# Two cross-attention layers on one core: query parts stored in 8 DMAs and loaded in 3, a row tile's products in parts, row turns one slot on, a last row tile in two column halves

## The chip, the cores and the metric

The kernel runs on 1 core of a Trainium2 chip. The metric is the device time of one launch in microseconds (us). The kernel before takes 1469.72 us, the median of 3 runs (1467.17 to 1472.53). Below, PE is TensorE (matmuls), DVE is VectorE, ACT is ScalarE, POOL is GpSimd, and SP is SyncE, which here only issues DMAs.

## The reference, cut to what matters

```python
def layer0(x, ctx):                        # x (8,100,512), ctx (8,722,512), H = 16 heads of 32
    qn, kn = layer_norm(x) * g1 + b1, layer_norm(ctx) * g1 + b1
    Q, K, V = qn @ wq + bq, kn @ wk + bk, kn @ wv + bv
    out = softmax(Q @ K.T / sqrt(32)) @ V
    x = x + out @ wo + bo
    y = layer_norm(x) * g2 + b2
    return x + gelu(y @ w1 + b1_) @ w2 + b2_
def layer1(q, ctx):                        # H = 16 heads of 64, no biases
    qh, kh, vh = q @ Wq, ctx @ Wk, ctx @ Wv
    out = softmax(qh @ kh.T / 8 - 2) @ vh @ Wfc + q
    return layer_norm(out) * gamma + beta
return layer1(layer0(x, ctx), ctx)
```

## The kernel before

Every fp32 operand of a matmul is split into two fp16 parts (high and low), and a product is three fp16 matmuls: high by high, high by low, low by high.

**Stages.** Attention 0 (0 to 537 us), the two MLP products (537 to 693), attention 1 (693 to 1468). Both attentions are `attention(nc, layer, ...)`. In layer 0 a unit is one of the 8 batches with its 16 heads in 4 groups of 4; in layer 1 there are 16 units (batch, half of the heads) with 2 groups. The work runs in steps: step s projects keys and values of unit s, computes scores and softmax of unit s - 1, and ends what is left of unit s - 2. A step has 24 slots in layer 0 (4 groups times 6 key tiles) and 12 in layer 1, and `Slots` is the table that says in which slot each piece stands. Every engine has its own loop over the same slots, in the same order (`step`), and the engines meet only in semaphores, so an engine that waits in a slot holds everything behind it.

**Scores.** `max_scores` makes a head's scores for the row maximum, `take_max` (DVE) reduces them, `max_transposes` and `place_max` bring the maximum into the query stack; `scores` makes the scores again, turned; `exp` and `prob_hi` (ACT) and `prob_lo` (POOL, in the last groups of layer 0 and in half of layer 1's tiles DVE) make the probabilities' parts; `times_v` multiplies by V. The first `max_scores` of unit u stands in slot 18 of step u. It waits for the unit's queries (`q_loaded`) and for the stacked keys of the first 8 heads (`stacked[0]`).

**The SP queue.** SP issues its DMAs in one written order. Before the steps of layer 0: `store_queries(m)` for four tiles (8 DMAs each: for each of 4 heads the high part, written twice, and the low part), the last two context tiles of batch 2, `queries_stored` (waits until the stores have landed), `place_onehot([1])`, `store_ctxT(1)` (the turned context of batch 1 to DRAM, 1444 KB, for layer 1). Then for unit 1: `load_q` (1 DMA over 96 partitions), `stack_k(.., 0)` and `stack_k(.., 1)` (12 DMAs each), more context tiles, `store_rstd`, `load_rrow`, and so on. Context tile (2, 5) waits until DVE has taken the statistics of tile (2, 1).

**Rows of layer 0.** The output projection, residual and second norm of row tiles 0 to 4 (128 rows each) are done inside the last steps: `row_products` (12 matmuls), `row_sum` with statistics, `row_power_of` (POOL), `row_centre`, `row_final`, `row_hi`, `row_lo`, `row_turn` (8 transposes), `row_copy`. `row_base` gives each tile's first slot, counted from the start of step 7, and `row_acc` to `row_turn` the offsets from it. Tile 4 has base 45, slot 21 of step 8; its bias is added by DVE at the head of its `row_sum`. Step 8 computes no projections any more, step 9 is the last group's `times_v` and the last output turn, and then comes a barrier and the MLP.

**Rows of layer 1.** `close_rows(T, half)` multiplies a row tile by half of Wfc (12 matmuls). In the last step (17) tiles 5 and 6 are left: both halves of tile 5 and the first of tile 6 stand in slot 5, behind the last `times_v`, and the second half of tile 6 in slot 9, behind the last output turn. `sum_rows` and `finish_rows` (DVE) end a tile, and SP stores it.

Of the kernel before, what the change touches and what calls it, by code (L numbers as in the profile page):

```python
# [25 lines left out]
P = 128  # L26
B, SQ, SK, E = 8, 100, 722, 512
ROWS = B * SQ
# [452 lines left out]
class Slots:  # L481
# [4 lines left out]
    def __init__(self, layer):  # L486
# [28 lines left out]
        self.row_base = [3, 9, 15, 21, 45]  # L515
        self.row_place = [4, 9, 13, 17, 18]
        self.row_acc, self.row_sum, self.row_pow, self.row_centre, self.row_final, self.row_hi, self.row_lo, self.row_turn = 0, 2, 3, 3, 4, 5, 7, 8
# [41 lines left out]
def attention(nc, layer, ctx_d, ctxT_d, q_d, w_k, w_v, kb_col, vb_row, ident, ident16, eps, score_bias, outT,  # L559
# [21 lines left out]
    NQ = 1 if layer == 0 else 3  # L581
    QM = queries[1].shape[3] // P
    QPER = 2 * HPT if layer == 0 else 2
# [3 lines left out]
    with Scope(nc, f"attn{layer}") as sc:  # L587
# [132 lines left out]
        if layer == 1:  # L720
# [4 lines left out]
            row_stats, row_mv = sc.sb("row_stats", [P, RT, 6]), sc.sb("row_mv", [P, RT, 2])  # L725
# [57 lines left out]
        def row_bank(T):  # L783
            return (p_proj, p_max)[T // 2 % 2][:, T % 2, :]
# [24 lines left out]
        def _(sp):  # L809
# [33 lines left out]
            def load_q(u, par, b):  # L843
                if not (isinstance(u, int) and u < 2):
                    sp.wait_ge(sc_ready, NSLOT * (u - 1))
                h0 = 0 if layer == 0 else NH * par
                if layer == 0:
                    sp.dma_start(qstack[0][:96, par], q_d[:, h0:h0 + NH, bass.ds(b * SQ, SQ)]).then_inc(q_loaded[par], 16)
                else:
                    part = lambda a: q_d[a, h0:h0 + NH, :, bass.ds(b * SQ, SQ)].rearrange("h p r -> p h r")  # L850
                    sp.dma_start(qstack[0][:DK, par], part(0)).then_inc(q_loaded[par], 16)
                    sp.dma_start(qstack[0][DK:, par], part(0)).then_inc(q_loaded[par], 16)
                    sp.dma_start(qstack[1][:DK, par], part(1)).then_inc(q_loaded[par], 16)
# [18 lines left out]
            def store_queries(m):  # L872

                if layer == 1:
                    sp.wait_ge(q_lo_made, 2 * m + 2)
                if layer == 0:
                    for j in range(HPT):
                        head, rows = HPT * m + j, slice(DK * j, DK * j + DK)
                        sp.dma_start(q_d[0:2 * DK, head, :].rearrange("(o p) (n r) -> p o n r", o=2, n=2),
                                     q_rows(0, m)[rows].rearrange("p (o n) r -> p o n r", o=1).to_broadcast([DK, 2, 2, QHALF])  # L880
                                     ).then_inc(q_stored[m % RING], 16)
                        sp.dma_start(q_d[2 * DK:, head, :].rearrange("p (n r) -> p n r", n=2), q_rows(1, m)[rows]).then_inc(q_stored[m % RING], 16)
                else:
                    for a in range(2):
                        sp.dma_start(q_d[a, HPT * m:HPT * m + HPT].rearrange("h p (n r) -> (h p) n r", n=2), q_rows(a, m)).then_inc(q_stored[m % RING], 16)
# [37 lines left out]
            if layer == 0:  # L923
                def unit(u, prep):
# [32 lines left out]
                    stack_k(u, u % 2, 1)  # L957
                    if u + 2 < U:
# [66 lines left out]
            if layer == 0:  # L1025
                store_ctxT(1)
# [32 lines left out]
        def _(pe):  # L1059
# [139 lines left out]
            def row_products(T):  # L1199
# [4 lines left out]
                pe.wait_ge(proj_freed, row_use(T) - 1)  # L1204
                if T == EARLY - 1:
                    pe.wait_ge(max_made, U * NG * HG)
                last_batch = (r0 + r - 1) // SQ
                pe.wait_ge(misc_freed, sl.misc_count(last_batch + 2, ("out", 0)))
                for k in range(ET):
# [3 lines left out]
                last.then_inc(proj_ready, 1)  # L1213
# [12 lines left out]
            def close_rows(T, half):  # L1226
# [15 lines left out]
                for k in range(ET):  # L1242
                    for i, (a, b) in enumerate(PARTS):
# [1048 lines left out]
```

## Time and profile before

| | us |
|---|---|
| median of 3 runs | 1469.72 (1467.17 to 1472.53) |
| the profiled execution, its own time | 1469.81 |
| its span | 1468.0 |
| PE busy | 1376.9 (94%) |
| DVE busy | 881.4 (60%) |
| ACT busy | 684.9 (47%) |
| POOL busy | 445.5 (30%) |
| mean granted PE clock | 0.982 |

The profile is one execution; its own time is 1.81 us over its span. A row of the timeline gives start, duration, engine, line of the kernel, operation, the tile written and those read, the count of instructions merged in it, and in brackets the idle time just before with what ended it. Matmuls are pipelined, so the work of PE is read from start to start.

### The profile page before, as it was taken

Reading aid. Unit: us, or ns where it says so; the run is one execution under the profiler, and the core shown is the slowest. Engines: PE = TensorE matmul, PEld = TensorE weight load, DVE = VectorE, ACT = ScalarE, POOL = GpSimd, SP = SyncE. Lnnn points to the kernel's source line nnn. Section 1 sums busy time; section 2 is a strip of 40 time slices with the busy share of each in tenths; the row PEclk is TensorE's granted clock in tenths of the full one; section 3 lists DMA queues with packets and bytes.
Section 4 is the critical chain, followed back from the end, with each engine's and each line's share of the span. In section 5 each row is a group of like instructions: output and inputs, shape, how many; then the busy total and the mean of one; then the engine's idle time right before and its main releaser. Section 6 shows DMA issues by size and latency. Waiting matters only on the chain.

```text
span 1468.0 us, 31527 instructions
## 1 busy us (share of the span) xinstructions
PE 1376.9 (94%) x12841; PEld 877.1 (60%) x12841; DVE 881.4 (60%) x1574; ACT 684.9 (47%) x1322; POOL 445.5 (30%) x493
## 2 busy tenths in 40 slices
PE   6988999999998879999999999999999999999997
PEld 4555666666655545544556666666666666666654
DVE  6777778878878748434435544454544445555564
ACT  3556567666755635221224444444444444444431
POOL 3125566666666731200001111112111111211223
PEclk9999999999999879999999999999999999999999
DMA  8226443343454035132433334123333322333421
GB/s 259 65 65 163 138 134 81 117 127 95 139 140 111 9 97 186 58 108 79 145 81 70 102 70 110 41 54 97 70 102 70 103 48 47 104 71 89 99 69 37
DMA packets 118205, 141.38 MB, mean 96 GB/s; under 512 B 49949, under 2 KB 92461, under 8 KB 116013
## 3 DMA queue, kind: packets, MB, share of 16 engines
q1 hardware_dynamic: 116873, 137.10, 34.4%
q8 instruction: 102, 1.67, 0.5%
q10 hardware_dynamic: 1188, 2.27, 0.5%
q14 instruction: 42, 0.34, 0.1%
HBM read 63.15 MB, written 22.17 MB: 58 GB/s over the span
## 4 chain that ended last, share of the span: by engine, by line
PE 47%; DVE 3%; issue 1%; ACT 1%; POOL 0%; POOLq 0%; ACTq 0%
PE attn_p_proj L1103 17%; PE attn_p_proj L1098 14%; PE attn_p_max L1125 3%; PE attn_p_sc L1314 2%; PE attn_p_sc L1156 2%; PE attn_p_sc L1155 2%; PE attn_p_pv L1184 1%; PE attn_p_proj L1244 1%; PE attn_p_pv L1183 1%; PE attn_p_pv L1185 1%; DVE attn_nmax L1692 1%; PE attn_p_max L1244 1%; ACT attn_probs L1460 1%; DVE attn_knat L1725 1%; ACT attn_knat L1489 0%
## 5 line engine op out<-in xcount | busy, mean ns | idle before, releaser
L1692 DVE TENSOR_REDUCE attn_nmax<-attn_p_max 100x1 f32<-100x722 f32 x250 | 226.3, 905 | 143.5 <-PE attn_p_max L1125 141.2
L799 POOL TENSOR_TENSOR attn_probs<-kernel_w_first,attn_probs 128x400 f16<-128x400 f32 x96 | 90.6, 943 | 673.4 <-ACT attn_probs L1460 673.4
L1103 PE MATMUL attn_p_proj<-kv_w_v,attn_ctxT 128*128 128x512 f16 (+1 forms) x1152 | 264.3, 379 | 0.0
L1450 ACT ACTIVATE kernel_w_first<-attn_p_sc,attn_score_bias 128x400 f32<-128x400 f32 x192 | 113.5, 591 | 307.9 <-PE attn_p_sc L1156 307.9
L1098 PE MATMUL attn_p_proj<-attn_ctxT,kv_w_k 128*128 128x361 f16 x1536 | 249.1, 317 | 4.1 <-DVE attn_knat L1725 3.5
L799 POOL TENSOR_TENSOR attn_probs<-attn_p,attn_probs 128x400 f16<-128x400 f32 x186 | 197.8, 1070 | 167.9 <-ACT attn_probs L1460 167.0
L1098 PEld LDWEIGHTS attn_p_proj<-attn_ctxT,kv_w_k 128*128 128x128 f16 x1536 | 144.6, 97 | 88.6 <-DVE attn_knat L1725 9.7
L1103 PEld LDWEIGHTS attn_p_proj<-kv_w_v,attn_ctxT 128*128 128x128 f16 (+1 forms) x1152 | 110.3, 101 | 111.1
L1450 ACT ACTIVATE attn_p<-attn_p_sc 128x400 f32<-128x400 f32 x192 | 96.4, 502 | 154.3 <-PE attn_p_sc L1152 151.6
L1103 PE MATMUL attn_p_proj<-l_w_v,attn_ctxT 128*128 128x512 f16 (+1 forms) x576 | 133.6, 382 | 1.9 <-DVE attn_vbuf L1731 1.8
L1098 PE MATMUL attn_p_proj<-attn_ctxT,kernel_w_first 128*128 128x361 f16 x768 | 127.9, 317 | 0.0
L1725 DVE SCALAR_TENSOR_TENSOR attn_knat<-attn_p_proj,attn_knat 128x361 f16<-128x361 f32 x128 | 68.3, 533 | 70.1 <-ACT attn_knat L1489 69.6
L1731 DVE SCALAR_TENSOR_TENSOR attn_vbuf<-attn_p_proj,attn_vbuf 128x512 f16<-128x512 f32 x96 | 66.2, 690 | 63.3 <-ACT attn_vbuf L1498 61.6
L1460 ACT CAST attn_probs<-attn_p 128x400 f16<-128x400 f32 x192 | 98.8, 519 | 0.0
L1460 ACT CAST attn_probs<-kernel_w_first 128x400 f16<-128x400 f32 x192 | 98.8, 515 | 0.0
L1098 PEld LDWEIGHTS attn_p_proj<-attn_ctxT,kernel_w_first 128*128 128x128 f16 x768 | 71.7, 97 | 37.8 <-issue 1.1
L1156 PE MATMUL attn_p_sc<-kernel_w_first,attn_kstack_b 72*128 72x100 f16 (+1 forms) x768 | 94.0, 208 | 0.0
L1155 PE MATMUL attn_p_sc<-kv_w 128*128 128x100 f16 (+1 forms) x768 | 93.5, 208 | 0.0
L799 DVE TENSOR_TENSOR attn_probs<-kernel_w_first,attn_probs 128x400 f16<-128x400 f32 (+1 forms) x96 | 55.2, 575 | 62.7 <-ACT attn_probs L1460 62.7
L1103 PEld LDWEIGHTS attn_p_proj<-l_w_v,attn_ctxT 128*128 128x128 f16 (+1 forms) x576 | 56.1, 102 | 59.6 <-DVE attn_vbuf L1731 2.6
L1489 ACT ACTIVATE attn_knat<-attn_p_proj 128x361 f16<-128x361 f32 x128 | 60.6, 473 | 62.5 <-PE attn_p_proj L1098 62.5
L1183 PE MATMUL attn_p_pv<-attn_vbuf,attn_probs 128*128 128x65 f16 (+1 forms) x768 | 84.9, 194 | 2.0 <-DVE attn_probs L799 2.0
(259 smaller groups left out, 2595.9 us busy)
## 6 DMA issues: line engine op xcount, KB each, us to landing
kv_w<-attn_knat SPq DMA_DIRECT2D x128, 180.5 KB, 3.5
attn_kstack<-attn_knat SPq DMA_DIRECT2D x192, 90.2 KB, 2.2
ctx_turned<-attn_ctxT SPq DMA_DIRECT2D x8, 1444.0 KB, 8.1
attn_ctxT<-ctx_turned SPq DMA_DIRECT2D x8, 1444.0 KB, 8.4
attn_kstack_b<-attn_knat SPq DMA_DIRECT2D x64, 180.5 KB, 3.6
attn_c<-in_ctx_dram SPq DMA_DIRECT2D x35, 256.0 KB, 3.2
kv_w_v<-in_L_xattn_w_dram SPq DMA_DIRECT2D x7, 1024.0 KB, 5.4
q_parts<-attn_probs SPq DMA_DIRECT2D x16, 200.0 KB, 2.5
```

The lines of the kernel that those rows point to most:

```text
L799: eng.tensor_tensor(probs[:r, g % 2, 1, t, :HG * SQ], p32[:r, t % 3, :], probs[:r, g % 2, 0, t, :HG * SQ], ALU.subtract).then_inc(p_lo_mad ...
L1098: last = pe.matmul(bank[:, :HALF], w_k[:, wa, k, c0 + m * P:c0 + (m + 1) * P], ctxT[:, cpar, ca, k, n * HALF:(n + 1) * HALF], **flags)
L1103: last = pe.matmul(bank[:r, :], ctxT[:, cpar, ca, k, P * t:P * t + r], w_v[:, wa, k, c0:c0 + E], **flags)
L1155: pe.matmul(out, kstack[0][:, par, h, P * t:P * t + r], qstack[0][:, par, h, :], start=True, stop=False)
L1156: last = pe.matmul(out, kstack[1][:MR + 2 * HG, par, h, P * t:P * t + r], qstack[1][:MR + 2 * HG, par, h, :], start=False, stop=True)
L1183: pe.matmul(p_pv[:, o:o + OC], ph, v[:, :OC], start=first, stop=False)
L1450: act.activation(p32[:r, t % 3, :], p_sc[:r, t % 2, :HG * SQ], ACT.Exp, bias=bias_col[:r, 0:1] if score_bias else 0.0).then_inc(exp_made, 1)
L1460: act.copy(probs[:r, g % 2, 0, t, :HG * SQ], p32[:r, t % 3, :]).then_inc(p_hi_made, 1)
L1489: act.activation(knat[:, m, 0, cols], src, ACT.Identity, scale=1.0 / WS).then_inc(k_hi_made, 1)
L1692: dve.tensor_reduce(nmax[:SQ, hh:hh + 1], max_banks(u, g, hh)[:SQ, :, :HALF], AX.XY, ALU.max, negate=True).then_inc(max_made, 1)
L1725: dve.scalar_tensor_tensor(knat[:, m, 1, cols], p_proj[:, a % 2, :HALF], 1.0 / WS, knat[:, m, 0, cols], ALU.mult, ALU.subtract).then_inc(p ...
L1731: dve.scalar_tensor_tensor(vbuf[:r, par, t, :, DK + 1:], p_proj[:r, use(u, a) % 2, :].rearrange("p (h d) -> p h d", d=DK), rstd[:r, par, t ...
```

## The change

1. **Queries of layer 0.** The DRAM tensor is now two parts by head (`q0_parts`), as in layer 1. `store_queries` issues 2 DMAs a tile, 8 in all, instead of 32. `load_q` issues 3 DMAs of 32 partitions for a unit (the high part twice, the low part once) instead of 1 of 96.
2. **`store_ctxT(1)`** moves from before the units to behind unit 1's second `stack_k`.
3. **Row turns of layer 0** stand one slot on (`row_turn` 8 to 9), and `row_copy` with them.
4. **Row tile 4**: base 45 to 42; its 12 matmuls are done 3 each in slots 16 to 19 of step 8, its bias is added in slot 17, its sum in slot 20, its turn in slot 3 of step 9.
5. **Layer 1**: `close_rows(5, 0)` moves from slot 5 to slot 0 of step 17. Tile 6 is computed in two halves of 256 columns in two banks, and its sum and statistics are taken for each half.

```diff
-        self.row_base = [3, 9, 15, 21, 45]
+        self.row_base = [3, 9, 15, 21, 42]
+        self.last_acc = {16: 0, 17: 1, 18: 2, 19: 3}
+        self.last_bias_t = 17
-        ... self.row_turn = 0, 2, 3, 3, 4, 5, 7, 8
+        ... self.row_turn = 0, 2, 3, 3, 4, 5, 7, 9
@@ load_q
-                if layer == 0:
-                    sp.dma_start(qstack[0][:96, par], q_d[:, h0:h0 + NH, bass.ds(b * SQ, SQ)]).then_inc(q_loaded[par], 16)
+                low = qstack[0][2 * DK:3 * DK, par] if layer == 0 else qstack[1][:DK, par]
+                sp.dma_start(qstack[0][:DK, par], part(0)).then_inc(q_loaded[par], 16)
+                sp.dma_start(qstack[0][DK:2 * DK, par], part(0)).then_inc(q_loaded[par], 16)
+                sp.dma_start(low, part(1)).then_inc(q_loaded[par], 16)
@@ store_queries
-                    for j in range(HPT):
-                        ...
+                for a in range(2):
+                    sp.dma_start(q_d[a, HPT * m:HPT * m + HPT].rearrange("h p (n r) -> (h p) n r", n=2), q_rows(a, m)).then_inc(q_stored[m % RING], 16)
@@ unit (SP, layer 0)
                     stack_k(u, u % 2, 1)
+                    if u == 1:
+                        store_ctxT(1)
@@ step (PE)
-                    if sl.row_tile(s, j, sl.row_acc) is not None:
+                    if layer == 0 and s == U - 1 and sl.row_tile(s, j, sl.row_acc) is not None:
                         row_products(sl.row_tile(s, j, sl.row_acc))
+                    if layer == 0 and s == U and j in sl.last_acc:
+                        row_products(EARLY - 1, range(sl.last_acc[j], sl.last_acc[j] + 1))
+                    if layer == 1 and s == U + 1 and j == 0:
+                        close_rows(RT - 2, 0)
                     if layer == 1 and s == U + 1 and j == PV_T + HG - 1:
-                        close_rows(RT - 2, 0)
                         close_rows(RT - 2, 1)
@@ row_cols
+            if T == RT - 1:
+                return [(slice(E // 2 * i, E // 2 * (i + 1)), p_max[:, i, :E // 2]) for i in range(2)]
@@ sum_rows
+                for i, (cols, bank) in enumerate(row_cols(T)):
+                    dve.wait_ge(rows_ready, T + i + 1)
+                    dve.scalar_tensor_tensor(res[T][:r, cols], bank[:r], 1.0 / WS, res[T][:r, cols], ALU.mult, ALU.add).then_inc(rows_summed, 1)
+                    dve.wait_ge(rows_summed, T + i + 1)
+                    dve.bn_stats(row_stats[:r, T + i, :], res[T][:r, cols]).then_inc(row_stats_made, 1)
@@ step (DVE)
+                    if layer == 0 and s == U and j == sl.last_bias_t:
+                        last_row_bias(EARLY - 1)
```

SP's queue from the end of the query stores to unit 1's keys, before; the first row is the last of 32 stores (`q_stack`), `attn_c` are context tiles, `attn_kstack<-attn_kstack` is `place_onehot`, `ctx_turned` is `store_ctxT(1)`, `attn_qstack<-q_stack` is `load_q(1)`, and the last row the 24 DMAs of `stack_k`.

```order
L882 DMA q_stack<-attn_kstack 32x800
L817 DMA attn_c<-in_ctx_dram 128x512
L817 DMA attn_c<-in_ctx_dram 82x512
L921 DMA attn_kstack<-attn_kstack 8x2888 x4
L836 DMA ctx_turned<-attn_ctxT 128x5776
L848 DMA attn_qstack<-q_stack 96x16x100
L899 DMA attn_kstack<-attn_knat 32x2x722 x24
```

The same stretch after:

```order
L879 DMA q_parts<-attn_kstack 128x800 x8
L821 DMA attn_c<-in_ctx_dram 128x512
L821 DMA attn_c<-in_ctx_dram 82x512
L915 DMA attn_kstack<-attn_kstack 8x2888 x4
L853 DMA attn_qstack<-q_parts 32x16x100
L854 DMA attn_qstack<-q_parts 32x16x100
L855 DMA attn_qstack<-q_parts 32x16x100
L893 DMA attn_kstack<-attn_knat 32x2x722 x24
L840 DMA ctx_turned<-attn_ctxT 128x5776
```

32 stores have become 8, one query load three, and the 1444 KB store stands behind the 24 key DMAs.

DVE at the end of step 8 and in step 9 before: `attn_ctxT<-attn_ctxT,attn_rrow` is the bias of row tile 4, `attn_probs` is `prob_lo`, `attn_ctxT<-attn_p_proj` the head of `row_sum`, `82x400` the last tile of the last group.

```order
L1786 TENSOR_TENSOR attn_ctxT<-attn_ctxT,attn_rrow 128x512
L1789 SCALAR_TENSOR_TENSOR attn_ctxT<-attn_p_proj,attn_ctxT 128x512
L1791 BN_STATS attn_stats<-attn_ctxT 128x6
L1793 BN_AGGR attn_mv<-attn_stats 128x2
L1795 TENSOR_SCALAR attn_mid_rstd<-attn_mv 128x1
L799 TENSOR_TENSOR attn_probs<-attn_p,attn_probs 82x400
```

After, the end of the same stretch:

```order
L1804 SCALAR_TENSOR_TENSOR attn_c<-attn_ctxT,attn_mv 128x512
L803 TENSOR_TENSOR attn_probs<-attn_p,attn_probs 128x400
L1811 SCALAR_TENSOR_TENSOR attn_c<-attn_c,attn_mid_rstd,attn_ctxT 128x512
L1741 COPY attn_pv_sb<-attn_p_pv 100x260
L1743 RECIPROCAL attn_orecip<-attn_pv_sb 100x4
L803 TENSOR_TENSOR attn_probs<-attn_p,attn_probs 82x400
```

The bias and the sum with its statistics stood ahead of the last `prob_lo`; now they are slots earlier, and `row_centre` and `row_final` stand ahead of it instead.

PE at the end of layer 1 before: `60x512` is row tile 5, `100x512` tile 6, `attn_misc` the last output turn.

```order
L1244 MATMUL attn_p_proj<-kernel_w_qo,kernel_x_parts 60x512 x12
L1244 MATMUL attn_p_proj<-kv_w_k,attn_out_o_upper 60x512 x12
L1244 MATMUL attn_p_max<-kernel_w_qo,kernel_x_parts 100x512 x12
L1196 MATMUL attn_misc<-kernel_ident,kv_w 128x100 x8
L1244 MATMUL attn_p_max<-kv_w_k,attn_out_o_upper 100x512 x12
```

After, the same place; tile 5's first half has gone ahead of the 72 matmuls of `times_v` that stand before these rows:

```order
L1241 MATMUL attn_p_proj<-kv_w_k,attn_out_o_upper 60x512 x12
L1241 MATMUL attn_p_max<-kernel_w_qo,kernel_x_parts 100x256 x24
L1190 MATMUL attn_misc<-kernel_ident,kv_w 128x100 x8
L1241 MATMUL attn_p_max<-kv_w_k,attn_out_o_upper 100x256 x24
```

## Rows read from the trace of the kernel before

**Rows 1.** Waits of PE, whole run; engine, tile, line <- releaser: us, times, longest
```profile
PE attn_misc L1133 <- DVE attn_nmax_parts L1701: 9.2, 17, 2.5
...
PE attn_misc L1223 <- DVE attn_cparts L1815: 5.6, 5, 2.0
PE attn_p_max L1125 <- issue: 5.3, 1, 5.3
PE attn_p_pv L1180 <- DVE attn_probs L799: 4.9, 1, 4.9
```

**Rows 2.** Timeline of SP, 104 to 150 us; start, duration, engine, line, transfer
```profile
105.25 0.59 SPq L879 DMA_DIRECT2D q_stack<-attn_kstack  x1
105.88 0.42 SPq L882 DMA_DIRECT2D q_stack<-attn_kstack  x1
...
125.53 2.77 SPq L921 DMA_DIRECT2D attn_kstack<-attn_kstack  x4
...
130.54 18.87 SPq L899 DMA_DIRECT2D attn_kstack<-attn_knat  x24
```

**Rows 3.** Layer 1's query stores and loads; ns min/median/max, first and last start
```profile
L885 SPq DMA_DIRECT2D q_parts<-attn_probs x16: 512/619/1435, 701.1 to 730.0; - x16
...
L853 SPq DMA_DIRECT2D kernel_w_first<-q_parts x16: 634/635/1576, 736.1 to 1361.0; - x16
```

**Rows 4.** Timeline of DVE, 112 to 116 us; start, duration, line, tiles
```profile
113.23 0.68 DVE L1650 BATCH_NORM_STATS2 attn_stats<-attn_c 128x6 f32<-128x512 f32 x1
...
115.56 0.96 DVE L1684 SCALAR_TENSOR_TENSOR attn_knat<-attn_kscaled,l_kb_col,attn_knat 128x722 f16<-128x722 f32 x1
```

**Rows 5.** Timeline of PE, 125 to 150 us, around the wait of step 1
```profile
125.09 0.49 PE L1125 MATMUL attn_p_max<-attn_kstack,attn_qstack 96*100 96x361 f16 x2
...
128.79 0.51 PE L1125 MATMUL attn_p_max<-attn_kstack,attn_qstack 96*100 96x361 f16 x2
...
143.35 0.81 PE L1125 MATMUL attn_p_max<-attn_kstack,attn_qstack 96*100 96x361 f16 x2 [5.33 <-issue]
...
149.29 0.47 PE L1125 MATMUL attn_p_max<-attn_kstack,attn_qstack 96*100 96x361 f16 x2
```

**Rows 6.** DMA issues; count, KB each, median us to landing
```profile
kv_w<-q_parts SPq DMA_DIRECT2D x32, 100.0 KB, 3.0
...
attn_qstack<-q_stack SPq DMA_DIRECT2D x7, 300.0 KB, 8.3
...
ctx_turned<-attn_ctxT SPq DMA_DIRECT2D x8, 1444.0 KB, 8.1
```

**Rows 7.** Timeline of DVE in step 8, behind the row turn
```profile
491.49 0.91 DVE L1692 TENSOR_REDUCE attn_nmax<-attn_p_max 100x1 f32<-100x722 f32 x1
```

**Rows 8.** Timeline of PE in step 8, row tile 4's products
```profile
519.12 3.35 PE L1211 MATMUL attn_p_proj<-kernel_w_qo,kernel_x_parts 128*128 128x512 f16 x12
522.31 0.35 PE L1152 MATMUL attn_p_sc<-attn_qstack,attn_kstack 104*128 104x100 f16 x4
```

**Rows 9.** Windows of step 8; length, busy us by engine, clock, DMA
```profile
506.50:520.00 13.50, 11.25 (x126) 8.88 (x127) 7.27 (x13) 9.85 (x22) 9.73 (x13) 0.51 0.01 2
```

**Rows 10.** Timeline of DVE before layer 0's last V product
```profile
524.68 1.30 DVE L1786 TENSOR_TENSOR attn_ctxT<-attn_ctxT,attn_rrow 128x512 f32<-128x512 f32 x1
...
527.83 0.56 DVE L799 TENSOR_TENSOR attn_probs<-attn_p,attn_probs 82x400 f16<-82x400 f32 x1
```

**Rows 11.** Timeline of PE at the end of layer 1
```profile
1444.82 0.19 PE L1183 MATMUL attn_p_pv<-attn_vbuf,attn_probs 128*128 128x65 f16 x1 [2.03 <-DVE attn_probs L799]
...
1448.47 2.90 PE L1244 MATMUL attn_p_proj<-kernel_w_qo,kernel_x_parts 128*60 128x512 f16 x12
1451.21 2.75 PE L1244 MATMUL attn_p_proj<-kv_w_k,attn_out_o_upper 128*60 128x512 f16 x12
```

**Rows 12.** Timeline of DVE in layer 1's last row tile
```profile
1460.54 0.69 DVE L1821 SCALAR_TENSOR_TENSOR attn_ctxT<-attn_p_max,attn_ctxT 100x512 f32<-100x512 f32 x1 [2.23 <-PE attn_p_max L1244]
```

**Rows 13.** Windows of layer 1's last V product
```profile
1444.90:1448.50 3.60, 3.60 (x73) 3.51 (x73) 2.77 (x6) 0.00 (x0) 1.94 (x2) 0.56 0.19 73
```

More of the change, by code:

```diff
@@ L514, in __init__ @@
         self.row_bias = [3, 8, 13, 20]
[L515 removed]
+        self.row_base = [3, 9, 15, 21, 42]
+        self.last_acc = {16: 0, 17: 1, 18: 2, 19: 3}
+        self.last_bias_t = 17
         self.row_place = [4, 9, 13, 17, 18]
[L517 removed]
+        self.row_acc, self.row_sum, self.row_pow, self.row_centre, self.row_final, self.row_hi, self.row_lo, self.row_turn = 0, 2, 3, 3, 4, 5, 7, 9
         self.shared_lo = {(last, g, t) for g in (2, 3) for t in (1, 3, 5)} if layer == 0 else set()
@@ L580, in attention @@
     NSTACK = 3 * HPT
-    NQ = 1 if layer == 0 else 3
+    NQ = 3
     QM = queries[1].shape[3] // P
-    QPER = 2 * HPT if layer == 0 else 2
+    QPER = 2
     NSLOT = sl.n
@@ L1197, in out_transposes, with row_products @@
                 last.then_inc(misc_ready, 1)
-            def row_products(T):
+            def row_products(T, ks=range(ET)):
                 r0, r = ROW0[T], RROWS[T]
@@ L1203, in row_products @@
                     pe.wait_ge(next_lo_made, ET)
[L1204 to L1209, printed above, removed]
+                if ks[0] == 0:
+                    pe.wait_ge(proj_freed, row_use(T) - 1)
+                    if T == EARLY - 1:
+                        pe.wait_ge(max_made, U * NG * HG)
+                    last_batch = (r0 + r - 1) // SQ
+                    pe.wait_ge(misc_freed, sl.misc_count(last_batch + 2, ("out", 0)))
+                for k in ks:
                     for i, (a, b) in enumerate(PARTS):
@@ L1241, in close_rows @@
                 _src, w_hi, w_lo = next_weights[half]
-                for k in range(ET):
-                    for i, (a, b) in enumerate(PARTS):
-                        last = pe.matmul(row_bank(T)[:r], outT[half][:, a, k, r0:r0 + r], (w_hi, w_lo)[b][:, k, :],
-                                         start=(half == 0 and k + i == 0), stop=(half == 1 and k == ET - 1 and i == 2))
-                if half == 1:
-                    last.then_inc(rows_ready, 1)
+                for cols, bank in row_cols(T):
+                    for k in range(ET):
+                        for i, (a, b) in enumerate(PARTS):
+                            last = pe.matmul(bank[:r], outT[half][:, a, k, r0:r0 + r], (w_hi, w_lo)[b][:, k, cols],
+                                             start=(half == 0 and k + i == 0), stop=(half == 1 and k == ET - 1 and i == 2))
+                    if half == 1:
+                        last.then_inc(rows_ready, 1)
             def turns(s, kind, j):
```

46 lines of the change are left out of this document (15 added, 31 removed).

## The prediction, made before the changed kernel ran

> **What bounds the kernel now.** I read first the whole run's waits of PE, because the page puts PE at 94% busy: what PE waits for is nearly all that can be won [rows 1]. Three of those rows, and one wait of the timeline, bear on the edits. One wait of 5.3 us stands before `max_scores` and its releaser is given only as "issue". One of 4.9 us stands before layer 0's last `times_v`, released by DVE's `prob_lo`. Five waits, 5.6 us in all, stand before `row_turn`. One of 2.0 us stands before layer 1's last `times_v` [rows 11]. Together this is some 18 us of 1470, and no edit touches the MLP or the steady steps of layer 1. Then I read the timeline around each wait, by engine, to see what ended it and what comes after it, and the windows for the granted clock there.
>
> **Step 1, the SP queue.** PE starts `max_scores(1, 0)` at 143.35 after 5.33 us of waiting, so it asked at 138.0 [rows 5]. It needs 12 key DMAs, and SP began those at 130.54; 24 take 18.87 us to issue, so 12 take 9.4 and the last goes out at 140.0 [rows 2]. It landed when PE went on, 3.4 us later. What held SP is ahead: its stores run from 105.25 in steps of 0.46 us (0.42 and the gap), and `place_onehot` begins only at 125.53 [rows 2].
>
> After the change: 8 stores at layer 1's median of 0.62 us are 5.0 us (bounds 4.1 and 11.5 by the row's shortest and longest) [rows 3], so they end at 110.3. Context tile (2, 5) then waits for DVE's second statistics of that step, 113.23 plus 0.68 [rows 4]; `place_onehot` takes 2.8 [rows 2] and ends at 116.9; three loads at 0.63 are 1.9 us [rows 3]; the key DMAs could go at 118.8. They also wait for the second key tile's low part, made at 115.56 plus 0.96 [rows 4], so that is no bound. Twelve at 9.4 us and a landing of 3.4 give 131.6, 6.4 us before PE asks. The wait goes. The 1444 KB store and two more issues no longer stand in between, and even at the longest store of 11.5 us the keys land in time.
>
> What goes with the wait is a stretch at 1.2 GHz. The same work, two `max_scores` matmuls, scores, a context turn and a value projection, takes 3.70 us from 125.09 to 128.79 and 5.94 from 143.35 to 149.29 [rows 5]: 2.24 us more, behind an idle PE. Gone with its cause, this gives 5.33 + 2.24 = 7.6 us. What is late next: DVE and ACT caught up in those 5 us; 17 waits on the split maximum cost 9.2 us in all, 0.5 each [rows 1], and I let one and a half of them show: 0.8. **Term A: 6.8 us** (5.5 to 7.6).
>
> The Trainium skill ("DMA: Bandwidth & Descriptors", the section on the anatomy of one DMA) gives a sequencer's dispatch as some 50 ns and puts the fixed cost of a DMA in its completion. By that price 24 fewer issues would bring the keys only 1.2 us sooner, and PE would still wait 4.1. The trace does not agree: SP's row says 0.46 us an issue [rows 2], nine times that, and it decides.
>
> **Query loads in three.** For units 2 to 7 SP issues 2 more DMAs, 1.3 us a unit. Layer 1 loads the same way, 100 KB in 3.0 us to landing, where the one load of 300 KB took 8.3 [rows 6]. Keys of a unit are asked for 18 slots after its query load is issued, two thirds of a step of 52 us, so neither the issue nor the landing shows. Cost 0, between 0 and what the slow rival says.
>
> **Row turns one slot on.** Of the 5.6 us, 5.1 are in steps 7 and 8 (the fifth wait, 0.5, is tile 4's in step 9, below). But there DVE is full: the `take_max` at 491.49, just behind the 2.0 us wait, shows no idle time before it [rows 7], so a PE that goes on arrives at that maximum earlier and waits there. I take a quarter, **term B: 1.2 us** (0 to 5.1). ACT's `row_copy` moves by a slot with it and no bank's next user is nearer than three slots.
>
> **Row tile 4.** Its 12 matmuls stand from 519.12 to 522.31, 3.19 us in slot 21 [rows 8]. In slots 16 to 19 the clock is at half rate (0.51 in the window to 520.0) [rows 9]. A 512-column matmul costs about 0.22 there at full rate (2.74 us for 12 [rows 11]) and 0.43 at half, so 12 cost 5.2. PE was idle 2.25 of 13.5 us of that window [rows 9], about 1 us in these slots, which they fill. So slot 22 would come 5.2 - 1.0 - 3.2 = 1.0 later; but as 3.2 us of work at half rate is then pushed behind 520.0, where the rate is full, it takes back 1.6. Net 0.6 sooner.
>
> Then the chain to `times_v`: DVE takes bias, sum and statistics from 524.68 to 527.83 before the last `prob_lo` [rows 10], 3.15 us that are now slots earlier. In their place come `row_final` on DVE and `row_hi` on ACT ahead of the last cast. The trace has no such pair at this place; bounded by 0 (hidden under the exponentials) and by three 512-wide operations at 0.69 [rows 12], 2.1. I take 0.9, since the centring lies under ACT's own work. Last, tile 4's turn no longer waits behind `times_v`, 0.5 less 0.1 for its own time inside it. **Term C: 0.6 + 3.15 - 0.9 + 0.4 = 3.3 us** (0.5 to 6). The upper end is a half-rate stretch that ends sooner, since PE has fewer gaps.
>
> **Layer 1's end.** One half of tile 5 lasts 1448.47 to 1451.21, 2.74 us [rows 11]. PE is idle 2.03 us before 1444.82, so it can start at 1442.8 and end at 1445.5; `times_v` begins 0.7 later than now. `times_v` took 3.65 us at a clock of 0.56 [rows 11, 13], 2.05 at full rate, and the half rate came right behind the idle stretch that is now filled. So the second half of tile 5 starts at 1445.5 + 2.05 = 1447.6 and not at 1451.21: 3.6 us. If the clock falls all the same, 2.0.
>
> Tile 6 in halves: 24 matmuls of 256 columns for 12 of 512, in two passes. No row has this shape; a price by columns makes it equal, and the price of a whole 512 each would add 2.7 a pass. I take equal, since a matmul of 12 merged ones here goes by its columns. At the end DVE's sum takes 0.69 [rows 12] and the statistics alike; at half the columns I take 0.42 each, between half and whole, 0.5 less in all. **Term D: 4.1 us** (2 to 4.3).
>
> **The sum.** 6.8 + 1.2 + 3.3 + 4.1 = 15.4 us against the profiled execution's own 1469.8 (span 1468.0 and 1.8 around it), which is 0.1 from the median of the runs: **1454.4 us**. The lower ends sum to 8.0 (1461.8), the upper ends to 23.0 (1446.8).
>
> **Rivals.**
>
> *Tail of layer 0 not won.* At half rate 12 matmuls cost 5.2, PE's idle time there is spread over more slots than four, and `row_hi` on ACT holds the last cast until DVE's `row_final` is ready. For it: POOL, DVE and ACT take turns in step 8. Against it: the 3.15 us of DVE are gone in any case. With C at 0.5: 1457.2.
>
> *The large store stands in the way.* `store_ctxT(1)` goes out at about 138 and takes 8.1 us to landing [rows 6]. Step 2 then needs the first tiles of batch 3 and the row of scales, whose DMAs are issued behind it. If these land after step 2 asks, PE waits up to 2 us: 1456.4. Against it: step 2 begins 6 slots of 2.2 us after 138.0, at 151, and 138 + 8.1 is 146. The Trainium skill (the same page, on queues, rings and completion order) says that each engine takes a ring's descriptors in order, so by it every load behind this store does wait for it; no row here shows whether they overtake.
>
> *The waits go whole.* Row turns leave 3 us more than I take, and half-rate stretches in steps 8 and 9 shorten with the idle time: C and B together 5.5 us better, 1449. For it: the clock is at half rate behind the idle stretches before 143.35 and 1444.82 [rows 5, 13]. Against it: DVE at 491.49.
>
> *Stores are not what holds the keys.* SP may wait for the parts of the last query tile and not for its own issues. Then only that tile's stores shrink, 8 of 0.46 to 2 of 0.62, 2.4 us; the large store's 0.6 goes, three loads add 0.4: the keys land 2.6 us sooner, PE still waits 2.7, and the half rate stays. A is 2.6 and the time 1458.6; with B, C and D at their low ends 1464.7. Against it: the stores follow each other with 0.04 us between them [rows 2].
>
> *Slower: the narrow query loads.* Each of the three covers 32 partitions. If each took as long as the one of 300 KB, 8.3 us [rows 6], the three would hold the ring 25 us. In step 1 the keys would then land at 118.8 + 25 + 3.4 = 147, 3.9 us after today's start: A is -3.9. In each of 6 further steps the last two context tiles, issued 5 us behind the loads, would land about 2 us after ACT asks. 1469.8 + 3.9 + 12 - 8.6 = 1477. It decides from about 17 us for the three. Against it: 3.0 us each in layer 1.
>
> **How the numbers follow.** Forecast 0.5; tail not won 0.15; large store 0.1; waits go whole 0.15; stores do not hold the keys 0.07; slower 0.03. The range runs from 1446.5 to 1461.5 and holds the first four but for their edges, and most of the fifth. About 0.3% (4.4 us) is what a measurement of this kernel can tell from no change; below 1465.3 is faster. Of the fifth case 0.04 lies within 0.3%: all low ends, and a microsecond or more for the 14 added loads. So faster 0.93, same 0.04, slower 0.03.
>
> **What the profile will show.** SP's first key DMA of unit 1 near 119 and no wait over 1 us before `max_scores` there; step 1 about 52 us long and no half-rate stretch in it. Waits before `row_turn` near 0 but longer ones before `max_scores` in steps 7 and 8. The last `times_v` of layer 0 about 2.9 us sooner, counted from slot 16. In layer 1, tile 5's first half in front of `times_v` with the clock at full rate, and two short sums at the very end. I am wrong if step 1 still has the wait, if a wait on the scales or on context tiles appears in step 2, or if slots 16 to 21 grow by more than 3 us.

## The result: 9 us faster, where 15 were forecast

The changed kernel takes 1461.4 us, the median of 4 runs (1459.97 to 1462.69), against 1471.12 for the kernel before in the same comparison. The ratio is 0.9938 with a 95% interval of [0.9914, 0.9961], or 9.1 us (5.7 to 12.6). A second comparison gave 1460.5 us and 0.9942 [0.9920, 0.9964], or 8.5 us. The forecast was 15.4 us, 1454.4 with a range of 1446.5 to 1461.5; the measured time stands at the slow edge of that range (all four terms at their low ends would give 1461.8). The sign was right, the size was 1.7 times too large, and two steps behind it were wrong: what holds unit 1's keys and how long the wait on them mostly is (term A), and what is left of layer 0's end behind the MLP (term C).

### The profile page after: what moved, and what is told of

Read it like the earlier page. It is cut to its first block, busy times and chain, and to the rows that moved or that the text cites. A ratio compares the mean times of both kernels' runs of the same rounds, so it can differ in the third digit from the quotient of the medians.

```text
span 1460.9 us, 31567 instructions
## 1 busy us (share of the span) xinstructions
PE 1378.4 (94%) x12865; PEld 876.8 (60%) x12865; DVE 881.4 (60%) x1576; ACT 686.5 (47%) x1322; POOL 448.4 (31%) x493
## 4 chain that ended last, share of the span: by engine, by line
PE 47%; DVE 3%; issue 1%; ACT 1%; POOL 0%; POOLq 0%; ACTq 0%; DVEq 0%
PE attn_p_proj L1097 17%; PE attn_p_proj L1092 14%; PE attn_p_max L1119 3%; PE attn_p_sc L1314 2%; PE attn_p_sc L1150 2%; PE attn_p_sc L1149 2%; PE attn_p_pv L1178 1%; PE attn_p_proj L1241 1%; PE attn_p_pv L1177 1%; PE attn_p_pv L1179 1%; DVE attn_nmax L1692 1%; PE attn_p_max L1241 1%; DVE attn_knat L1725 1%; ACT attn_probs L1460 1%; ACT attn_knat L1489 0%
## 5 line engine op out<-in xcount | busy, mean ns | idle before, releaser
L1092 PE MATMUL attn_p_proj<-attn_ctxT,kernel_w_first 128*128 128x361 f16 x768 | 131.1, 322 | 0.0
```

The lines of the kernel that those rows point to most:

```text
L1092: last = pe.matmul(bank[:, :HALF], w_k[:, wa, k, c0 + m * P:c0 + (m + 1) * P], ctxT[:, cpar, ca, k, n * HALF:(n + 1) * HALF], **flags)
```

## The profile after

The page of the changed kernel: the span, the busy times, and the granted clock in 40 slices.

```profile
span 1460.9 us, 31567 instructions
...
PE 1378.4 (94%) x12865; PEld 876.8 (60%) x12865; DVE 881.4 (60%) x1576; ACT 686.5 (47%) x1322; POOL 448.4 (31%) x493
...
PEclk9999999999999779999999999999999999999999
```

The profiled execution took 1462.69 us, 7.1 less than that of the kernel before. PE's busy share has not changed. The waits of PE, whole run, with the same columns as [rows 1]:

```profile
PE attn_misc L1127 <- DVE attn_nmax_parts L1701: 9.2, 17, 2.5
...
PE attn_p_max L1119 <- DVE attn_nmax L1692: 7.2, 13, 1.1
...
PE attn_p_pv L1174 <- DVE attn_probs L803: 5.7, 1, 5.7
...
PE attn_misc L1219 <- DVE attn_cparts L1816: 1.4, 1, 1.4
```

Of the waits in [rows 1], the one of 5.3 us before `max_scores` is gone. Of the five before `row_turn` one is left. The wait of 4.9 us before layer 0's last `times_v` is not shorter but longer, 5.7. The second row above grew too. In the kernel before it read:

```profile
PE attn_p_max L1125 <- DVE attn_nmax L1692: 5.6, 12, 1.1
```

SP's timeline in step 1, which answers to [rows 2]; `q_parts<-attn_kstack` are the query stores, the L821 row the context tiles, `attn_kstack<-attn_knat` the keys.

```profile
107.15 4.04 SPq L879 DMA_DIRECT2D q_parts<-attn_kstack  x8
111.29 6.47 SPq L821 DMA_DIRECT2D attn_c<-in_ctx_dram  x2
117.95 2.77 SPq L915 DMA_DIRECT2D attn_kstack<-attn_kstack  x4
120.76 0.82 SPq L853 DMA_DIRECT2D attn_qstack<-q_parts  x1
...
123.20 18.57 SPq L893 DMA_DIRECT2D attn_kstack<-attn_knat  x24
141.82 0.59 SPq L840 DMA_DIRECT2D ctx_turned<-attn_ctxT  x1
```

The stores go out in 4 us instead of 17, but SP comes to the keys only 7 us sooner than in [rows 2]: the context tiles hold it from 111.3 to 117.8. The 1444 KB store stands behind the keys now.

The end of step 8, in answer to [rows 10]: PE, then DVE, then ACT (`attn_c` is row tile 4 on its way through the norm, `82x400` the last tile of probabilities).

```profile
516.46 0.38 PE L1146 MATMUL attn_p_sc<-attn_qstack,attn_kstack 104*82 104x100 f16 x4 [0.49 <-ACT attn_p L1450]
...
522.90 0.21 PE L1174 MATMUL attn_p_pv<-attn_vbuf,attn_probs 128*128 128x65 f16 x1 [5.69 <-DVE attn_probs L803]
```

```profile
516.17 0.68 DVE L1790 SCALAR_TENSOR_TENSOR attn_ctxT<-attn_p_proj,attn_ctxT 128x512 f32<-128x512 f32 x1
...
519.59 1.52 DVE L1811 SCALAR_TENSOR_TENSOR attn_c<-attn_c,attn_mid_rstd,attn_ctxT 128x512 f32<-128x512 f32 x1
...
522.22 0.57 DVE L803 TENSOR_TENSOR attn_probs<-attn_p,attn_probs 82x400 f16<-82x400 f32 x1 [0.56 <-ACT attn_probs L1460]
```

```profile
518.63 0.50 ACT L1450 ACTIVATE attn_p<-attn_p_sc 82x400 f32<-82x400 f32 x1 [0.99 <-POOL attn_probs L803]
...
521.14 0.62 ACT L1521 CAST attn_cparts<-attn_c 128x512 f16<-128x512 f32 x1 [1.60 <-DVE attn_c L1811]
521.67 0.52 ACT L1460 CAST attn_probs<-attn_p 82x400 f16<-82x400 f32 x1
```

The sum no longer stands ahead of the last `prob_lo`. In its place `row_final` does, and takes 1.52 us, and ACT's `row_hi` waits 1.60 us for it (521.14) with the last cast behind it (521.67). PE waits till 522.90.

The windows of the MLP's first 12 us, in the kernel before and in the changed one, and of 12 us around the start of the MLP's second product in the changed one. The clock is the third number from the end.

```profile
537.77:549.77 12.00, 12.00 (x59) 6.26 (x60) 5.02 (x6) 4.72 (x5) 2.71 (x2) 0.87 0.87 247
```

```profile
531.55:543.55 12.00, 12.00 (x53) 5.91 (x54) 3.66 (x5) 4.72 (x5) 3.52 (x2) 0.75 0.90 299
601.38:613.38 12.00, 9.43 (x45) 4.47 (x43) 3.78 (x8) 1.79 (x3) 3.96 (x5) 0.86 0.24 73
```

The MLP starts 6.2 us sooner (531.55 against 537.77), but at a clock of 0.75 instead of 0.87, and 53 matmuls stand in these 12 us where 59 did.

The end of layer 1, PE and DVE, which answers to [rows 11] and [rows 12]:

```profile
1439.43 2.78 PE L1241 MATMUL attn_p_proj<-kernel_w_qo,kernel_x_parts 128*60 128x512 f16 x12
...
1444.46 2.78 PE L1241 MATMUL attn_p_proj<-kv_w_k,attn_out_o_upper 128*60 128x512 f16 x12
1447.17 2.82 PE L1241 MATMUL attn_p_max<-kernel_w_qo,kernel_x_parts 128*100 128x256 f16 x24
```

```profile
1453.87 0.43 DVE L1823 SCALAR_TENSOR_TENSOR attn_ctxT<-attn_p_max,attn_ctxT 100x256 f32<-100x256 f32 x1 [0.35 <-PE attn_p_max L1241]
1454.33 0.43 DVE L1826 BATCH_NORM_STATS2 attn_row_stats<-attn_ctxT 100x6 f32<-100x256 f32 x1
```

Tile 5's first half stands in the gap (1439.43), `times_v` follows without a wait, and the last sum and statistics take 0.43 us each instead of 0.69.

## Where the time went, section by section

Each kernel run below left a profile too, 14 in all with the first two. In each I took the same six places from the timelines, so that a section's length can be compared apart from what happened ahead of it. The places are starts of instructions: the exponentials of a slot on ACT, the first matmul of a stage on PE.

| section | as before | as changed | gain | forecast |
|---|---|---|---|---|
| slot 17 of step 1 to unit 1's first exponential | 21.80; 18.52, 18.66, 18.60, 18.31 | 14.57 to 14.59 (9 profiles) | 3.9 (7.2 in the first pair) | A: 6.8 |
| on to slot 6 of step 8 | 338.88 to 339.09 (6) | 338.41 to 338.49 (8) | 0.5 | B: 1.2 |
| on to the MLP's first matmul | 37.30 to 40.09, mean 38.4 (5) | 36.30 to 36.94, mean 36.6 (8) | 1.8 | C: 3.3 |
| MLP, to layer 1's first matmul | 155.80 to 156.55, mean 156.0 (5) | 156.59 to 158.70, mean 157.6 (8) | -1.6 | (in C) 0 |
| on to layer 1's last exponential | 748.68 to 749.48, mean 748.9 (5) | 748.68 to 749.62, mean 749.1 (8) | -0.3 | 0 |
| layer 1's last exponential to the end | 25.76 to 25.87 (5) | 21.91 to 21.93 (8) | 3.9 | D: 4.1 |

"As before" and "as changed" go by the edit that touches the section, whatever else a kernel has; the numbers in brackets count profiles, and the two experiments that alter a section otherwise (10 the last, 11 the third to fifth) are left out of its row. Of the first row 3.9 leaves out the first profile, 21.80. At unit 1's first exponential, which counts all that lies ahead of it, the five profiles with the wait stand at 158.5 to 160.3 us and the nine without at 154.7 to 156.5, 3.8 apart on the mean with the first profile in. The gains sum to 8.2 us, against 9.1 and 8.5 measured.

What the MLP gives back goes by how much of its start lies at half rate. In five profiles (the kernel before, 1, 3, 9, 11) that is 3.1 to 3.4 us, and the MLP takes 155.80 to 155.93. In five (2, 5, 6, 7, 8) it is 4.6 to 4.9, and the MLP takes 156.55 to 156.64. In four (the changed kernel, 4, 10, 12) it is 5.5 to 5.9, a stretch of 3.4 us at half rate in the second product comes to it, and the MLP takes 158.41 to 158.70. The second group has one kernel with the old rows (2). All of the second group also show 6.8 us at half rate at layer 1's start where the third has 3.4, and take 0.8 us more there (749.5 to 749.6 against 748.7).

## Experiments

**1. The kernel before, profiled again.** No edit.

> The kernel before, unchanged, profiled once more. Theory (the profile on which the prediction rests had PE 2 us ahead of what it mostly is when it comes to the wait for unit 1's keys, and the keys' landing does not move with PE): a half-rate stretch near 103 us, the wait before max_scores of step 1 about 3 us and not 5.3, its end again at 143.2 to 143.4, step 1 shorter by 3 us. Rival (the two kernels that showed this are different there, the profile of before is typical): 5.3 us again and no half-rate stretch near 103 us.

Measured: the wait is 2.96 us and not 5.33, and the stretch near 103 us is there. The wait ends at 142.55, 0.8 us sooner than in the first profile. The windows of 101 to 105 us, of the first profile and of this one, and PE's row in this one:

```profile
101.00:105.00 4.00, 3.81 (x30) 2.51 (x31) 2.91 (x7) 1.51 (x4) 0.00 (x0) 1.00 0.14 28
```

```profile
101.00:105.00 4.00, 3.62 (x17) 2.01 (x18) 2.49 (x7) 1.01 (x2) 0.00 (x0) 0.57 0.50 164
```

```profile
142.55 0.81 PE L1125 MATMUL attn_p_max<-attn_kstack,attn_qstack 96*100 96x361 f16 x2 [2.96 <-issue]
```

PE goes on at 142.55, and at 143.35, 143.18 and 143.31 in the three other profiles with 32 stores, the single load and the large store ahead of the keys, each time within 0.1 us of the 12th key's landing. PE asks at 138.0 in the first profile and at 139.6 to 140.5 in the others. So the wait takes up whatever PE loses ahead of it: of the first profile's 5.33 us, 2.2 to 2.5 were an early arrival, spent in waiting.

**2. The queries' edit alone**, and **3. one half of it alone**: the kernel before with the large store moved, and nothing else.

```diff
-            if layer == 0:
-                store_ctxT(1)
             for u in range(1 - layer, U):
@@ unit (SP, layer 0)
                     stack_k(u, u % 2, 1)
+                    if u == 1:
+                        store_ctxT(1)
```

> The kernel before with only the query stores and loads and the move of the large store. In the changed kernel the step with the wait became 7.2 us shorter, but a half-rate stretch of 1.7 us stood at 104 us where the kernel before had none, and layer 0 started 1.8 us later. Theory 1 (the edit gives its 7.2 us whole, and the two losses ahead of it are luck of the single run): ratio about 0.995, 7 us faster than the kernel before, and the losses come and go between profiles. Theory 2 (the edit causes the losses, since it alone touches this stretch): 3.7 us faster, ratio 0.9975, with the half-rate stretch at 104 us there again.

> The kernel before with one edit: store_ctxT(1) behind unit 1's keys. 32 stores and the single query load stay. Theory (the keys are late since 1444 KB stand in the queue ahead of them; the landing, not SP's issue, is what the wait ends on): the longest landing of a key DMA falls from 6 to 7 us to about 3, the wait before max_scores of step 1 (2.9 to 5.3 us) falls to 0 to 0.5, unit 1's scores start at 155 to 156 and not at 158.5 to 160.3, and the ratio is 0.9975 to 0.998, all that the queries' edit gave. Rival (the 300 KB load over 96 partitions, 10 us to landing, holds them): 1 to 3 us of the wait stay, ratio 0.999.

Measured: 1466.58 us and 0.9980 [0.9969, 0.9990] for the whole edit; 1466.38 us and 0.9980 [0.9966, 0.9994] for the move alone. Two lines give all that the queries' edit gives. The wait is gone in both. The size for (2) is that of its second theory, but not for its reason: the half-rate stretch at 104 us, which that theory laid to the edit, stands in the kernel before too when it is profiled again (experiment 1). In both, steps 2 to 8 are as long as before (338.9 us to slot 6 of step 8), so the large store behind the keys makes nothing late in step 2.

**4 to 6. Which part holds the keys.** The changed kernel with 32 stores (4; the count of stores that `queries_stored` awaits goes with it and is not shown), with the large store early (5), and with both (6).

```diff
@@ 4: store_queries, layer 0
-                for a in range(2):
-                    sp.dma_start(q_d[a, HPT * m:HPT * m + HPT].rearrange("h p (n r) -> (h p) n r", n=2), q_rows(a, m)).then_inc(q_stored[m % RING], 16)
+                    for j in range(HPT):
+                        for a in range(2):
+                            sp.dma_start(q_d[a, HPT * m + j].rearrange("p (n r) -> p n r", n=2),
+                                         q_rows(a, m)[DK * j:DK * j + DK]).then_inc(q_stored[m % RING], 16)
@@ 5: back ahead of unit 1
-                    if u == 1:
-                        store_ctxT(1)
+            if layer == 0:
+                store_ctxT(1)
```

> The changed kernel with 32 query stores again, one for each head and part, and all else as it is (three loads, the large store behind the keys). Theory (the number of SP's issues holds the keys): the stores take 15 us of SP again, max_scores of step 1 waits about 3 us again, and the whole is 3 to 4 us slower than the changed kernel, ratio to the kernel before 0.996 to 0.9965. Rival (the duplicated high part, the bytes or the large store held them): no wait, ratio 0.994 as in the changed kernel.

> The changed kernel with store_ctxT(1), 1444 KB, back in front of unit 1's query loads. Theory (only its issue counts, 0.6 us, and the keys have some 4 us to spare now): no wait before max_scores and no change, within 1 us of the changed kernel. Rival (its packets hold the queue in front of the keys): the keys land 8 us after they are issued instead of 2 to 3, PE waits 1 to 4 us in step 1, and the kernel is 2 to 5 us slower than the changed one.

> The changed kernel with 32 query stores and with the large store back ahead of the query loads; each of the two alone changed nothing. Theory (either edit is enough, so both undone bring the wait back): a wait of 2.5 to 3 us before max_scores of step 1, a longest key landing of 5 us or more, 3 to 4 us slower than the changed kernel, ratio 0.9965. Rival (what held the keys was the single query load, gone here too): no wait, ratio 0.994.

Measured: (4) 1461.24 us, 0.9942 [0.9926, 0.9957]; (5) 1460.64 us, 0.9939 [0.9923, 0.9955]; (6) 1464.85 us, 0.9965 [0.9951, 0.9979]. My theory for (4) fell; those for (5) and (6) held. SP's timeline of (4):

```profile
106.80 15.96 SPq L881 DMA_DIRECT2D q_parts<-attn_kstack  x32
...
128.86 16.21 SPq L899 DMA_DIRECT2D attn_kstack<-attn_knat  x24
145.12 0.59 SPq L840 DMA_DIRECT2D ctx_turned<-attn_ctxT  x1
```

The stores take 16 us again, and the keys begin at 128.86. In the kernel before, profiled again, they begin at 128.72. PE waited 2.96 us there and does not wait here. What differs is how the key DMAs go through, as the rows of the 24 show (ns min/median/max to issue one, then first and last start; us to landing below), first of the kernel before, then of (4), (5) and (3):

```profile
L899 SPq DMA_DIRECT2D attn_kstack<-attn_knat x24: 594/597/4596, 128.7 to 148.0; - x24
...
DMA to landing us min/median/max: 1.7/2.1/7.4
```

```profile
L899 SPq DMA_DIRECT2D attn_kstack<-attn_knat x24: 596/597/1368, 128.9 to 144.5; - x24
...
DMA to landing us min/median/max: 1.6/2.2/3.1
```

```profile
L893 SPq DMA_DIRECT2D attn_kstack<-attn_knat x24: 594/597/1422, 124.4 to 140.8; - x24
...
DMA to landing us min/median/max: 2.1/2.2/3.7
```

```profile
L899 SPq DMA_DIRECT2D attn_kstack<-attn_knat x24: 595/597/1582, 128.8 to 145.3; - x24
...
DMA to landing us min/median/max: 1.7/2.2/5.0
```

With the large store just ahead of them, one key DMA takes 4.6 us to issue and one 7.4 us to land. Without it (4), 1.4 and 3.1. With the single query load ahead and the large store behind (3), 1.6 and 5.0. `max_scores` needs 12 of them, and the 12th is in at 142.5, 138.2 and 139.2 us, from keys begun at 128.7 to 128.9 in all three. The first and the last differ by the large store alone, 3.2 us. In (5) the large store is ahead too, and SP is held right behind it:

```profile
118.94 0.50 SPq L840 DMA_DIRECT2D ctx_turned<-attn_ctxT  x1
...
120.81 1.90 SPq L854 DMA_DIRECT2D attn_qstack<-q_parts  x1
```

But with 8 stores ahead all of it comes 9 us sooner, and the 12th key is in at 134.5, some 5 us before PE asks. In (6) the same stands behind 32 stores:

```profile
128.05 0.44 SPq L840 DMA_DIRECT2D ctx_turned<-attn_ctxT  x1
128.53 1.00 SPq L853 DMA_DIRECT2D attn_qstack<-q_parts  x1
129.58 2.00 SPq L854 DMA_DIRECT2D attn_qstack<-q_parts  x1
131.62 1.82 SPq L855 DMA_DIRECT2D attn_qstack<-q_parts  x1
133.49 15.85 SPq L899 DMA_DIRECT2D attn_kstack<-attn_knat  x24
```

```profile
143.55 0.48 PE L1125 MATMUL attn_p_max<-attn_kstack,attn_qstack 96*100 96x361 f16 x2 [2.56 <-issue]
```

Behind the large store the second and third query load take 2.00 and 1.82 us to issue (0.84 and 0.49 in (4)), the keys begin at 133.49 and not at 128.86, and PE waits 2.56 us. So 32 stores alone leave the keys in time (4), the large store ahead of them alone does too (5), and the two together make them late (6). Either edit alone takes the wait away, and both together give no more than one. That the store's packets fill the queue is my reading of these rows; the single packets were not followed.

The Trainium skill ("DMA: Bandwidth & Descriptors", on queues, rings and completion order) says that each engine consumes a ring's descriptors in order. The trace fits that: 7.4 us to the latest landing behind the store, 3.1 without it. Landings do not keep the order: in (6) the first query load, issued behind the store, is in at 135.4 us, and the store at 136.0.

**7. The rows' edits alone** (row turns and row tile 4 on the kernel before), and **8. the row turns back** (`row_turn` 8 in the changed kernel).

> The kernel before with only the row turns a slot on and row tile 4 in parts and sooner. Theory 1 (the clock takes it back): the MLP starts about 2.5 us sooner, but its half-rate stretch reaches further into it, so that layer 1 starts only 1 us sooner: 1 us faster, ratio 0.9993. Theory 2 (the prediction's terms B and C, of which the profiled run showed too little by luck): 4.5 us faster, ratio 0.997.

> The changed kernel with the row turns back on their slot (row_turn 8). Theory (DVE bounds these steps): the waits before row_turn come back, but steps 7 and 8 up to their middle grow by only 0.3 to 0.7 us, time within 1 us of the changed kernel, ratio 0.994. Rival (term B as predicted or more): 1.2 to 3 us slower.

Measured: (7) 1468.82 us, 0.9993 [0.9981, 1.0005]; (8) 1461.33 us, 0.9944 [0.9924, 0.9964]. In (8) the waits before `row_turn` are all back:

```profile
PE attn_misc L1219 <- DVE attn_cparts L1816: 5.0, 4, 2.0
```

They cost 5.0 us there, and yet the section up to slot 6 of step 8 grew by only 0.4 to 0.5 us. So these waits of PE are not what bounds it, as the first theory said; that it is DVE is read from [rows 7] and from the waits on its maximum, which grew from 5.6 to 7.2 us, and was not tested by itself. In (7) the third and fourth section take 36.57 and 156.59, 193.2 us, against 194.4 on the mean of the profiles with the old rows; the 8 profiles with the new ones have a mean of 194.2. So the first theory held, in the whole time too, which is 1 us less (interval -0.7 to 2.8), and the second, 4.5 us, fell: the MLP starts 2.3 us sooner on the means (0.5 and 1.8), and what is left of the third section's gain behind the MLP is between 0 and 1 us.

**9. Layer 1's end alone**, and **10. tile 6 undivided** (the changed kernel with one range of columns for every tile).

```diff
@@ 10: row_cols
-            if T == RT - 1:
+            if False:
                 return [(slice(E // 2 * i, E // 2 * (i + 1)), p_max[:, i, :E // 2]) for i in range(2)]
```

> The kernel before with only layer 1's end: tile 5's first half in the gap, tile 6 in halves. Theory: 3.8 us faster, ratio 0.9974, as the last stretch of the two profiles differs, with no half-rate stretch behind 1442 us. Rival: the half rate moves to another place of the end and half of it is lost, 2 us, ratio 0.9986.

> The changed kernel with tile 6 of layer 1 undivided again. Theory by the prediction's own split of term D (3.6 for tile 5's first half in the gap, 0.5 for the halves): 0.5 us slower than the changed kernel. Rival (the halves do more, since the first half's sum lies beside the second half's products): 1 to 2 us slower.

Measured: (9) 1466.97 us, 0.9979 [0.9965, 0.9993]; (10) 1461.68 us, 0.9944 [0.9926, 0.9962]. The last section is 21.91 us in (9) against 25.8, and 22.43 in (10) against 21.92. So tile 5's first half is worth 3.4 and the division 0.5, close to the prediction's 3.6 and 0.5. The end of (10) has DVE's two long rows back:

```profile
1452.95 0.69 DVE L1823 SCALAR_TENSOR_TENSOR attn_ctxT<-attn_p_max,attn_ctxT 100x512 f32<-100x512 f32 x1 [2.31 <-PE attn_p_max L1241]
1453.68 0.69 DVE L1826 BATCH_NORM_STATS2 attn_row_stats<-attn_ctxT 100x6 f32<-100x512 f32 x1
```

**11. Row tile 4's last steps behind the last `prob_lo`.** The changed kernel with `row_final` and `row_hi` of tile 4 two slots and one slot on.

```diff
-    def row_tile(self, s, j, ahead):
+    def row_tile(self, s, j, ahead, late=0):
         base = (s - self.units + 1) * self.n + j - ahead
+        if late and self.layer == 0 and self.row_base[4] in (base, base - late):
+            return 4 if base - late == self.row_base[4] else None
@@ step (DVE), step (ACT)
-                        row_final(sl.row_tile(s, j, sl.row_final))
+                        row_final(sl.row_tile(s, j, sl.row_final, 2))
-                        row_hi(sl.row_tile(s, j, sl.row_hi))
+                        row_hi(sl.row_tile(s, j, sl.row_hi, 1))
```

> The changed kernel with row_final and row_hi of row tile 4 behind the last prob_lo of layer 0 instead of ahead of it. Theory (row_final and row_hi hold the last cast, as the changed kernel's timeline shows): the wait before the last times_v falls from 5.7 to about 3.5 us, the MLP starts 1.5 to 2 us sooner, and the whole is 1 to 2 us faster than the changed kernel (about 0.9930 of the kernel before). Rival (the last row turn becomes late instead, or the half-rate stretch reaches further into the MLP): same time as the changed kernel within 0.5 us.

Measured: 1459.65 us, 0.9929 [0.9909, 0.9949], the fastest of all kernels here. DVE, then PE, at that place:

```profile
518.89 0.95 DVE L805 TENSOR_TENSOR attn_probs<-attn_p,attn_probs 82x400 f16<-82x400 f32 x1
519.77 0.74 DVE L1813 SCALAR_TENSOR_TENSOR attn_c<-attn_c,attn_mid_rstd,attn_ctxT 128x512 f32<-128x512 f32 x1
```

```profile
519.94 0.22 PE L1176 MATMUL attn_p_pv<-attn_vbuf,attn_probs 128*128 128x65 f16 x1 [3.90 <-DVE attn_probs L805]
...
521.94 0.29 PE L1221 MATMUL attn_misc<-kernel_ident,attn_cparts 128*128 128x128 f16 x1 [0.52 <-DVE attn_cparts L1818]
```

`prob_lo` comes ahead of `row_final`, the wait is 3.90 us instead of 5.69, and the MLP starts 35.28 us after slot 6 of step 8 instead of 36.6 (36.30 at the least). In this profile the gain also outlasts the MLP (155.93), but it is one profile, the fastest of five executions by 3 us, and the only one of the 14 without a half-rate stretch at layer 1's start. That it beats the changed kernel is shown for this section, not for the total: the two intervals overlap.

**12. The changed kernel again**, as a control.

> The changed kernel once more, as a control beside the others. Theory (its profiled run had a half-rate stretch of 3.4 us in the MLP's second product and a late start that most runs don't have): the median 1460 to 1461.5, ratio 0.994, and a profile in which layer 0 starts about 1 us sooner. Rival: the same stretch at 608 us again.

Measured: 1460.5 us, 0.9942 [0.9920, 0.9964]. Layer 0 starts 1 us sooner, as expected, but the half-rate stretch of 3.4 us in the MLP's second product is there again. It is in four of the eight profiles with tile 4 as changed, and in none of the six others. The MLP is 1.9 us longer with it, some 1.5 of that for the stretch itself, and 0.8 comes back at layer 1's start. Why it comes there is open.

## Why the prediction was wrong in size

**Term A, 6.8 forecast, 3.9 found: the term that failed most.** The step that failed is its first sum, 5.33 + 2.24 = 7.6: the prediction read the length of a wait and of a half-rate stretch from one execution. In the three others of the same kind the wait is 2.9 to 3.2. Only what ends the wait is fixed, the landing of the keys at 142.5 to 143.3; its start moves with PE. The first profile had PE about 2 us ahead, 1.1 to 1.7 of it because the clock stayed full at 101 to 105 us where it fell in the others, and its half-rate stretch in step 1 was 6.8 us long where the others show 3.4. In the first pair the section shrank by 7.2 us, but the changed kernel came to it 3.5 us later, and 3.7 was left at unit 1.

**The step on what holds the keys was half wrong, and its result, no wait, was right.** "What held SP is ahead" is true of the stores, and a chain of issue and landing (12 at 9.4 us, 3.4 to land) gave the right end. But the issue was not at its own pace: one of the 24 took 3.6 us in the first profile, which stood hidden in the row's 18.87 us for 24 (at the median of 0.6 they would take 14.3). The prediction counted the large store at its issue alone, and gave the gain to the 24 stores saved; moving the large store gives it all without them (experiment 3). Its own rival on that store had the mechanism, and put it one step too late. The rival that the stores do not hold the keys had half of its title right, but by a wait for the last query tile that no run shows, and with 2.7 us of waiting left where none is.

**SP reaches the keys at 121.5 to 124.4, not at 118.8.** The context tile waited for DVE as said, but to between 115.9 and 117.8 and not to 114. Nothing hung on it, as the missing wait shows. The 0.46 us an issue held (15.96 us for 32, 4.04 for 8). It does not speak against the Trainium skill, though: the section that the prediction set it against ("DMA: Bandwidth & Descriptors", on the anatomy of one DMA) prices the path of DMAs issued from GpSimd, and these are issued from SP.

**Term B, 1.2 forecast, 0.5 found.** That PE would not gain what these waits cost was right. The waits of PE moved from `row_turn` to `max_scores` (5.6 to 7.2 us in the waits).

**Term C, 3.3 forecast, 1.8 found at the MLP's start, 0.2 at layer 1's first matmul and nothing at its last exponential.** Two things. The last `prob_lo` is held by `row_final` and `row_hi`, which I priced at 0.9 of a range up to 2.1; experiment 11 took 1.3 us out by moving them alone, so they cost that much more. And the gain stops at the MLP: it now starts deeper inside a half-rate stretch and does more of its work in it. That is 0.8 us in half of the profiles; in the other half it is 1.2, and the later stretch, whose cause is open, adds some 1.5. The prediction followed the clock up to the end of the layer and not beyond. Of the rivals "the tail of layer 0 not won", with a chance of 0.15, came nearest: it named `row_hi` as what holds the last cast.

**Term D, 4.1 forecast, 3.9 found**, with its split, the clock at full rate and the short sums as said.

The narrow query loads cost nothing, as forecast: from unit 1's first exponential to slot 6 of step 8 it is 338.92 us with three loads (2) and 338.89 with one (3). With the terms as found the sum is 8.2 us.

## What to carry to other kernels

A wait on a transfer with a fixed landing is a buffer: before it is priced, its end and the engine's arrival are to be read in several executions, since only the difference is won, and it takes up what comes ahead of it. Where a wait has two causes in series, undoing each alone in the changed kernel shows nothing; do one alone on the kernel before as well, and both together. A gain that ends inside a half-rate stretch is to be followed to the next stage, since the work that moves up is done at half rate.

## What was not expected of the hardware

- A large store in SP's queue delays not only landings but the issue of the DMAs behind it: 4.6 us for one key DMA (1.6 with that store moved away, experiment 3; median 0.60), 2.00 and 1.82 us for two query loads (0.84 and 0.49 in experiment 4).
- With the same instructions and the same idle time of 2.48 us ahead of it, the clock stayed at full rate in one profile (1.00 at 101 to 105 us) and fell within 3 us in the 13 others (0.57 in experiment 1's), which is worth 1.1 to 1.7 us at that place. Why it held once is open. Runs of one kernel spread over 10 us, from 1462.96 to 1473.26 for the kernel before, while the first and the last section as changed, in which PE runs at full rate, repeat within 0.02 us.
